# Planes of patches written out in DRAM, one transfer for a stack of patches, and the next pair's front end eight units earlier

## The reference

```
x = x + scale * conv3x3(sign(groupnorm(x)), sign(weight))
x = x + involution7x7(groupnorm(x))

involution(x): r   = relu(batchnorm(w_reduce @ x + b_reduce))       # 64 -> 16 channels, each pixel
               ker = w_span @ r + b_span                             # 49 x 16 weights, each pixel
               out[channel c of group g] = sum over 49 taps of xpad[c, pixel + tap] * ker[tap, g, pixel]
```

## Time and profile before

| | us |
|---|---|
| median of 3 runs | 1940.97 (1937.63 to 1954.17) |
| the profiled execution: its time | 1947.81 |
| the profiled execution: its span | 1945.9 |
| PE busy in the span | 1615.7 (83%) |
| DVE busy | 1377.2 (71%) |
| ACT busy | 1054.9 (54%) |
| POOL busy | 1016.5 (52%) |
| DMA engines, SP's queue | 73.1% of the span |
| DMA engines, ACT's queue | 10.2% of the span |

### The profile page before, as it was taken

How to read it: one execution, slowest core, us unless ns; L and a number is a source line. 1 busy time by engine, 2 the same in 40 slices (tenths; PEclk the granted TensorE clock), 3 DMA queues, 4 the chain that set the end, 5 groups by cost and what they waited for, 6 DMA issues and landing times.

```text
span 1945.9 us, 38822 instructions
## 1 busy us (share of the span) xinstructions
PE 1615.7 (83%) x15072; PEld 730.2 (38%) x15072; DVE 1377.2 (71%) x1699; ACT 1054.9 (54%) x758; POOL 1016.5 (52%) x904
## 2 busy tenths in 40 slices
PE   3488897979889798897978889798897978889785
PEld 2233443434344343343434344343343433344342
DVE  6476786858678686786858678676786858678574
ACT  2355566555656455565545656454565545656443
POOL 1145565454655555465554655555565454655573
PEclk8699998999999899998989999898998999999897
DMA  3669899797998979799797998979799797988992
GB/s 108 166 168 242 187 261 217 189 245 175 253 211 229 231 192 245 183 260 208 204 229 187 257 199 238 226 188 241 188 254 215 197 236 181 254 206 227 208 248 85
DMA packets 211592, 410.67 MB, mean 211 GB/s; under 512 B 83822, under 2 KB 131231, under 8 KB 207263
## 3 DMA queue, kind: packets, MB, share of 16 engines
q1 hardware_dynamic: 136144, 356.79, 73.1%
q10 hardware_dynamic: 75264, 51.39, 10.2%
HBM read 310.30 MB, written 84.93 MB: 203 GB/s over the span
## 4 chain that ended last, share of the span: by engine, by line
POOL 49%; issue 42%; PE 2%; SPq 2%; DVE 2%; DMA 2%; ACT 1%; POOLq 1%; ACTq 0%; DVEq 0%
POOL folded L361 49%; SPq L301 1%; PE ybank L508 1%; POOLq L360 1%; SPq L283 0%; DMA patches<-parts_dram 0%; PE ybank L567 0%; DMA xs<-x_dram 0%; DVE rowsums L730 0%; DVE prod L788 0%; DMA parts_dram<-parts 0%; PE ybank L537 0%; PE ybank L548 0%; ACT patches L428 0%; ACT sgn L381 0%
## 5 line engine op out<-in xcount | busy, mean ns | idle before, releaser
L361 POOL TENSOR_TENSOR folded<-prod 128x448 f32<-128x448 f32 x896 | 1010.8, 1141 | 911.7 <-DVE prod L788 910.9
L788 DVE TENSOR_TENSOR prod<-ybank,relu 128x896 f32<-128x896 f32 x896 | 960.9, 1088 | 405.7 <-PE ybank L567 336.3
L567 PE MATMUL ybank<-patches,wspan 128*64 128x448 f16 x7168 | 863.2, 383 | 240.8 <-ACT patches L428 106.0
L428 ACT ACTIVATE patches<-patches 96x1792 f16<-96x1792 f16 x448 | 736.6, 1689 | 554.7 <-DMA patches<-parts_dram 273.7
L567 PEld LDWEIGHTS ybank<-patches,wspan 128*64 128x64 f16 x7168 | 400.2, 117 | 757.2 <-issue 421.7
L508 PE MATMUL ybank<-sgn,convw 128*128 128x448 bf16 x1008 | 206.4, 358 | 21.4 <-ACT sgn L381 17.0
L585 PE MATMUL obank<-folded,esum 128*32 128x448 f32 x1792 | 214.8, 551 | 1.5 <-POOL folded L361 1.5
L578 PE MATMUL obank<-patches,wbias 128*32 128x448 f16 x3584 | 197.1, 363 | 0.0
L508 PEld LDWEIGHTS ybank<-sgn,convw 128*128 128x128 bf16 x1008 | 93.7, 98 | 135.3 <-issue 31.5
L578 PEld LDWEIGHTS obank<-patches,wbias 128*32 128x32 f16 x3584 | 87.1, 98 | 103.8 <-issue 50.9
L746 DVE SCALAR_TENSOR_TENSOR xs<-ybank,scale,xs 128x896 f32<-128x896 f32 x64 | 66.0, 1032 | 74.9 <-PE ybank L508 74.8
(11 more groups left out here) (90 smaller groups left out, 378.0 us busy)
## 6 DMA issues: line engine op xcount, KB each, us to landing
patches<-parts_dram SPq DMA_DIRECT2D x1120, 224.0 KB, 7.1
parts_dram<-parts SPq DMA_DIRECT2D x128, 256.0 KB, 5.4
xs<-x_dram SPq DMA_DIRECT2D x16, 1568.0 KB, 9.7
sums_dram<-osb ACTq DMA_DIRECT2D x112, 224.0 KB, 6.2
rows<-sums_dram ACTq DMA_DIRECT2D x112, 224.0 KB, 6.7
out_dram<-xs SPq DMA_DIRECT2D x16, 1568.0 KB, 5.9
relu<-blocks SPq DMA_DIRECT2D x256, 49.0 KB
patches<-gb_dram SPq DMA_DIRECT2D x1, 784.0 KB
```

Source lines behind the costliest of these rows:

```text
L361: pool.tensor_tensor(folded[:, u % 8, :], prod[:, u % 2, 0, :], prod[:, u % 2, 1, :], ALU.add).then_inc(fold_done, 1)
L428: act.activation(X2[0:COPIED_ROWS, e % 2, at], X1[0:COPIED_ROWS, e % 3, at], ACT.Copy).then_inc(copied, 1)
L567: mm = pe.matmul(bank("unit", p, n)[64 * t:64 * t + 64, h, 0:N], wspan[:, stack, g, h, :], of_group(e, stack, g), start=(stack == 0), stop ...
L788: dve.tensor_tensor(prod[:, u % 2].rearrange("m h (n c) -> m h n c", c=GC), bank("unit", p, n)[:, :, 0:N].rearrange("m h (n c) -> m h n c" ...
```

## The change

**DRAM layout.** `parts_out` now writes the planes out: each of the eight planes of the first stack stands in DRAM in its own row of 2,048 elements, beside the other seven (`planes_dram`), and the two planes that only the second stack has stand in a second tensor (`planes2_dram`). The same data is thus written several times, with another shift for each copy: ten rows for each partition and piece where there were four. Piece k = 0 takes ten transfers, the other pieces six each; before it was two for each piece.

**Reading.** The rows of a plane stand at every eighth partition in both stacks, so that `first_stack` is one transfer to 128 partitions. ACT copies all 128 rows of the second stack (in units 0, 1, 2, 3), and `second_stack` reads two planes of 16 rows over the copy. It waits for the copy first. In SP's list `first_stack` stands before `second_stack`.

**Order.** The front end's tables are eight units lower: the convolution at units 3, 4, 6, 9 where it was 11, 12, 14, 17, the transposes at 20, 22, 26, 28 where they were 28, 30, 34, 36, the reduction at 29 and 30. `totals`, `negative_mean` and `sign` moved to units 48 to 53 of the pair before. `gather` is in unit 4, and `rows` in unit 3, one block later. `rsum` has a tile of its own; it shared one with `blocks`, and the waits for that are gone. The input's load moved to block 4, behind `spread`.

```diff
-PLANES = (((0, 0, 32, 4), (0, 4, 0, 2), (0, 1, 33, 4), (1, 0, 96, 2),
-           (0, 2, 34, 4), (1, 1, 1, 2), (0, 3, 35, 4), (1, 2, 97, 2)),
-          ((0, 0, 32, 4), (0, 4, 0, 2), (0, 1, 33, 4), (0, 2, 34, 4), (0, 3, 35, 4),
-           (1, 3, 96, 2), (1, 4, 97, 2)))
+PLANES = (((0, 0), (0, 2), (0, 4), (1, 1), (0, 1), (0, 3), (1, 0), (1, 2)),
+          ((0, 0), (0, 2), (0, 4), (1, 3), (0, 1), (0, 3), None, (1, 4)))
+Q = 8
+LOADED = (3, 7)
+TOTALS_AT = {48: 0, 49: 1, 50: 2, 51: 3}
+MEAN_AT, SIGN_AT = 52, 53
+CONV_AT = {3: 0, 4: 1, 6: 2, 9: 3}
+VARIANCE_AT, AFFINE_AT = 10, 12
+T_AT = {20: 0, 22: 1, 26: 2, 28: 3}
+RED_AT = {29: 0, 30: 1}
+COPY_AT = {0: 0, 1: 1, 2: 2, 3: 3}
...
             def parts_out(p, k):
                 sp.wait_ge(low_done, 4 * p + k + 1)
...
-                for l in range(2):
-                    sp.dma_start(D[p % 2, l].rearrange("m (y h n) -> m y h n", y=2, h=4)[:, :, k, :],
-                                 Ev[:, l, k % 2]).then_inc(d_written[k], 16)
+                def run(dram, planes, q, l, y, shift, many):
+                    src = Ev[:, l, k % 2, y]
+                    if k == 0:
+                        for i in range(many):
+                            cut = BLOCK * (shift + i)
+                            sp.dma_start(dram[b, :, q + i, 0:4 * BLOCK - cut], src[:, cut:]).then_inc(d_written[k], 16)
+                        return
+                    dst = bass.AP(tensor=dram.tensor, offset=(128 * b * planes + q) * RUN + BLOCK * (4 * k - shift),
+                                  ap=[[planes * RUN, 128], [RUN - BLOCK, many], [1, 4 * BLOCK]])
+                    sp.dma_start(dst, src.unsqueeze(1).broadcast_to((128, many, 4 * BLOCK))).then_inc(d_written[k], 16)
+                run(D0, Q, 0, 0, 0, 0, 3)
+                run(D0, Q, 4, 0, 1, 0, 2)
+                run(D0, Q, 6, 1, 0, 0, 2)
+                run(D0, Q, 3, 1, 1, 0, 1)
+                run(D1, 2, 0, 1, 1, 1, 1)
+                run(D1, 2, 1, 1, 0, 2, 1)
...
             def first_stack(e):
...
-                for l, a, row, step in PLANES[0]:
-                    sp.dma_start(X1[row:row + 15 * step + 1:step, e % 3, :],
-                                 plane(e, l, a)).then_inc(first_in[e % 3], 16)
+                sp.dma_start(X1[:, e % 3, :].rearrange("p (j n) -> p j n", j=JX), stack(D0, e)).then_inc(first_in[e % 3], 16)
             def second_stack(e):
+                sp.wait_ge(copied, JX * (e + 1))
                 if e >= 2:
-                    sp.wait_ge(y_ready, GP * (e - 1))
                     sp.wait_ge(second_in[e % 2], SECONDLOAD * (e // 2))
...
+                for i, q in enumerate(LOADED):
...
+                    sp.dma_start(X2[q:128:Q, e % 2, :].rearrange("p (j n) -> p j n", j=JX), src).then_inc(second_in[e % 2], 16)
...
                     e = E * p + s
+                    if e + 2 < EALL:
+                        first_stack(e + 2)
                     if e + 1 < EALL:
                         second_stack(e + 1)
-                    if e + 2 < EALL:
-                        first_stack(e + 2)
                     if p + 1 < pairs:
-                        if s == 3:
+                        if s == 2:
                             parts_out(p + 1, 0)
                             parts_out(p + 1, 1)
-                        if s == 4:
+                        if s == 3:
                             parts_out(p + 1, 2)
                             parts_out(p + 1, 3)
+                        if s == 4:
                             spread(p + 1)
                     if s == 2 and p > 0:
                         store(p - 1)
-                    if s == 3 and p + 2 < pairs:
+                    if s == 4 and p + 2 < pairs:
...
-                act.activation(X2[0:COPIED_ROWS, e % 2, at], X1[0:COPIED_ROWS, e % 3, at],
-                               ACT.Copy).then_inc(copied, 1)
+                act.activation(X2[:, e % 2, at], X1[:, e % 3, at], ACT.Copy).then_inc(copied, 1)
```

94 lines of the change are left out of this document (48 added, 46 removed).

## The result

The changed kernel takes **2059.4 us** (2052.6 to 2060.0) against 1940.3, a ratio of 1.059 with a 95% interval of 1.054 to 1.065. The direction was forecast, the size was not: +119 us instead of +48. All ratios compare fast executions; a single one, of experiment 10's kernel, was slow (5124 us) and is left out.

A forecast was written before the change was run, and what follows sets the result against it. PE waits for a full line of transfers, 56.3 us, so block 6 starts at 106.1; with its 13.7 a pair takes 119.8, 3.1 more, +47 over 15 pairs. The forecast is 1941 + 48 = 1989 us, range 1885 to 2065.

The forecast's parts named there:

- the start of block 6: Block 6 starts 106.1 us after the pair: 37.0 + 11.4 + 56.3 + 1.4.
- slow writes: Rival: planes written at 219 GB/s, not 351; pieces take 22.8 us, 2118 in all; chance 0.12 together with slow stacks.
- slow single transfers: Rival: a first stack runs at 220 GB/s, 8.3 us, +10.2 a pair, 2142; chance 0.12 together with slow writes.
- PE may be three results ahead, which gives back some 2.4 us: 13.7: Block 6: DVE has 16.1 us of work against PE's 12.0; PE's lead cuts the block to 13.7.
- The line: All transfers from the first piece of planes to block 6's second stack pass one after another: 56.3 us.
- The stretch: Measured counterpart of the 56.3 us: from the first piece's issue to 1.4 us before PE starts block 6.
- the share of 0.56: The spread holds about half of the DMA engines while it runs, so its 13.5 us count as 6.
- block 4's undisturbed start, 66.6: The SP-bound case counts from block 4's start at 66.6 us; 33.4 us later, at 100.0, block 6 starts.
- The SP-bound case: Rival: SP's issuing from block 4 on sets block 6's start, 100.0; pair 113, total 1885, faster; chance 0.27.

The follow-up runs named there:

- experiment 10: The kernel of experiment 8 with the last piece of planes issued behind block 4's stacks instead of ahead of them: 1930.4 us, 0.994.
- experiment 6: The changed kernel without the four totals in block 6, so the sign uses an old mean: 2021.8 us, 1.043.
- experiment 1: The changed kernel with the spread issued behind block 5's stacks instead of behind block 4's: 1960.8 us, 1.011.
- exp. 3: The changed kernel writing only six of the ten rows of a partition and piece from the third pair on: 2014.8 us, 1.039.
- exp. 14: The changed kernel writing only four of the ten rows of a partition and piece from the third pair on: 2000.2 us, 1.028.
- experiment 11: The kernel of experiment 8 with eight of the spread's transfers behind block 5's stacks and eight behind block 6's: 1899.6 us, 0.980.
- experiment 2: The changed kernel with the second stack issued before the first stack in each block: 2164.4 us, 1.115.
- experiment 13: The old layout with the new tables, plus first stack ahead of second and the second waiting for ACT's copies: 2243.1 us, 1.156.
- experiment 8: The changed kernel with spread behind block 5's stacks, totals, mean and sign at units 43 to 51, block 2's store before second stack and pieces: 1907.8 us, 0.983.

## Why the prediction was right in direction and wrong in size

**The parts of it that held.** The wrong size comes from the pairs: 15 of them took 102 us more, where 47 were forecast. (The first unit's start moved by 13 us, 9 forecast; the last pair and the tail were 10 shorter, 9 forecast.) The starts of blocks 1 and 2 came within 0.5 us of the forecast, and the start of block 6 was forecast at 106.1 and is 107.6. These windows show the rates (the writes of planes, a first stack, the spread with ACT's transfers, then the load with block 7's first and block 6's second stack):

```profile
1041.00:1043.00 2.00, 1.72 (x10) 1.06 (x12) 0.00 (x0) 2.00 (x3) 0.00 (x0) 0.50 1.10 384
1048.00:1050.00 2.00, 2.00 (x24) 1.13 (x20) 1.32 (x3) 0.57 (x1) 1.46 (x3) 1.00 1.02 418
1056.00:1059.00 3.00, 3.00 (x22) 1.96 (x20) 1.81 (x2) 3.00 (x3) 1.04 (x1) 0.60 0.65 154
1060.00:1074.60 14.60, 7.37 (x88) 2.94 (x84) 6.14 (x6) 4.79 (x5) 7.32 (x7) 0.85 0.97 326
```

Planes were written at 384 GB/s (351 assumed) and a first stack ran at 418 (373 assumed) while nothing else passed. So the rivals of slow writes and of slow single transfers are both out.

**The step that failed: "PE may be three results ahead, which gives back some 2.4 us: 13.7."** Block 6 takes 16.1 to 16.2 us. That is 2.4 us a pair or 36 in all, the largest part of the 71 that the forecast lacks. DVE's work was summed at 16.1 us, and I took 2.4 off because PE may run ahead at the block's end. The trace shows what happens at both ends. PE starts block 6 after a wait, with DVE empty, and DVE's first product begins 1.7 us after PE:

```profile
1076.39 1.09 DVE L811 TENSOR_TENSOR prod<-ybank,relu 128x896 f32<-128x896 f32 x1 [8.78 <-PE ybank L590]
...
1089.70 2.08 DVE L811 TENSOR_TENSOR prod<-ybank,relu 128x896 f32<-128x896 f32 x2
```

From there DVE has no gap until 1091.8, 15.4 us, and PE starts the next pair at 1090.8, 1.0 us before that end: 1.7 + 15.4 - 1.0 = 16.1. Against the forecast the late first product costs 1.7, the lead at the end is 1.4 smaller, and the work is 0.7 less: 2.4. That DVE's work is the bound is shown by experiment 6 (without the totals, 13.9). The clock is not: here block 6 begins, after 7.3 us of waiting, at a granted clock of 0.50 (24 matmuls in 4.69 us at 1074.65), and in experiment 1 with a fast one (2.46 us), where DVE's first product came 1.0 us after PE, and the block took 16.2 us all the same.

**The line: near in its sum, by terms that cancel.** The prediction has "56.3 us of transfers in one line". The stretch measures 57.5 us at a DMA share of 0.95. What passed, as medians over 14 pairs, in us of all 16 engines' time, counted by queue and packet size:

```
                      forecast   changed   exp. 1   exp. 3   exp. 14
pieces of planes        14.2       15.0      15.0      9.1      6.0
store and load           8.0        8.6       8.7      9.1      9.1
first, second stacks    21.0       22.1      21.1     22.5     22.9
spread                   6          3.4       0.6      3.9      4.2
ACT's queue              7.1        5.3       5.7      5.6      6.0
idle                     0          2.9       0        4.2      5.5
stretch                 56.3       57.5      51.7     55.5     54.1
```

So the line was nearly full, as forecast, and it is luck that the sum is so close: the spread and ACT's queue were put 4.4 us too high, the rest 2.5 too low, and the 2.9 us of idle time were not in it. The spread came out at 6 because the share of 0.56 was read from a window in which most of its packets passed together with some of ACT's and of the pieces'; all its packets took 3.4 us in that pair of the kernel before, too. Block 6's start is 1.5 us later than forecast, 22 over the pairs.

**The order, which the sum left out.** Where the 2.9 us come from can be read from SP's queue. Block 5's first stack is late because of two pieces and the store ahead of it (the queue is full there, at 331 GB/s and a share of 1.00 in block 3), which makes the copies and block 5's second stack late; the spread's 12.2 us of issuing start only behind that, and near its end the queue runs empty (the window from 1056 on: a share of 0.65, of which the spread is 0.28 and ACT's queue 0.32). I had both links, the second as a rival that "decides where the line of 56.3 is shorter than 51". There I started it from block 4's undisturbed start, 66.6. Block 4 started at 73.9, and 73.9 + 33.4 = 107.3, with 107.6 measured. A queue and an issue order are not alternatives, of which the longer one counts. When bytes are taken out, the order keeps most of the time: in experiments 3 and 14 the pieces take 5.9 and 9.0 us less, and the stretch is 2.0 and 3.4 shorter.

**The rest of the 71 us.** The set-up lacks 4 us. Another 14 are no effect of the kernel: the median lies 7 above the profiled execution, where it was 7 below before. (The parts come to a little more than 71, since medians over pairs don't add up exactly.)

**The rivals.** The SP-bound case was right in naming the link and wrong in its sign, and so in its 1885 us (for which it also put block 6 at 13.0, where the sum has 13.7): SP's order alone doesn't set the time as long as the queue makes block 4 late. With the spread later (experiment 1) the queue alone is left.

**What the layout costs.** With the same tables and the spread in the same block: 2061 against 1941, 2059 against 1978, 1961 against 1918. With the order of experiment 11 it is the other way round, 1900 against 2001. So the cost is one of the layout together with its order, not of the layout as such. Each of these pairs differs in more than the planes: the units of the copies, of `gather` and of `rows` and the order in SP's list go with the stacks. Three things can cost, and only the first was measured by itself: 5.0 MB of planes instead of 2.1 a pair, just ahead of the stack that is waited for (experiment 14: 5.9 us of blocks 3 and 4, 3.2 of the pair); the second stack behind the copies and behind the next first stack; and SP's waiting for the copies, behind which all its other issues stand (experiments 2 and 13 show that such a wait can cost 5 and, with later copies, 17 us a pair). How much of the second and third is in the changed kernel stays open: no run has the new stacks without the wait, since the copy writes the rows that the second stack brings.

## What to carry to other kernels

A queue that is worked off in order has to be read twice: what it moves and when its issuer comes to each entry. Small transfers that nobody waits for yet (the spread: 12 us of issuing, 3.4 us of the engines' time) delayed a transfer that was waited for, and moving them a block later won 5% without changing any work. A saving in bytes is worth what the order lets through: of 9 us of writes, 3.4 arrived. A new wait ahead of a faster transfer can eat up what it saves; in experiment 2, where only the place of SP's wait for the copies changed, it cost 5%. Work that is moved into a block with little of PE's work (the totals in block 6) can bound that block: taking their 3.8 us away made it 2.2 us shorter. And a sum that comes out right is not yet an explanation: here two terms that were too high hid the gap.

## What the runs showed of the hardware

Four things I had not expected. First, issuing took longer when much stood ahead in the queue: six transfers of a piece took 3.69 us, and twelve took 12.01 us right after, with the store, a first stack and a piece ahead of them. Most of these twelve took 0.5 to 0.9 us each, but two took 2.86 and 2.32. In experiment 8, with the store gone from there, the same twelve took 9.7 us. Second, the writes were not slower with a step of 32 KB between partitions and with the same source written up to three times: 384 GB/s. Third, a single transfer to 128 partitions of rows of 3.6 KB ran at 418 GB/s, more than the 373 of the best 16-row transfers. Fourth, ten transfers with one row length a partition were issued in 4.79 us, 0.48 each, and six of the next piece in 0.62 each. A repeated source is not the reason: the three that have one took 0.38, 0.49 and 0.62 us, the three without 0.72, 0.68 and 0.59.
